# Weighing both halves of a gated chunk in one vector operation over two PSUM banks

## The chip, the cores and the metric

The kernel runs on one core of one Trainium2 chip. The metric is the device time of one launch in microseconds (us), and the time given for the kernel is the median of its runs. Beside them stands one profiled execution, from which all the rows below come.

## The reference

A stack of four layers works on `x` of 8 sequences x 128 tokens x 128 features. Each layer adds an attention (or recurrent) part and a feed-forward part, both behind a layer norm and scaled by `tanh` of a gain. The feed-forward part of the third layer is a mixture of 64 experts with 96 hidden features each, of which each token takes 8. It is the one that matters here; the kernel calls it the second mixture (m = 1; the first mixture, m = 0, is layer one's, and the third, m = 2, is layer four's).

```python
def _L2_ffn_ref(hidden_states, gate_w, w_gate, w_up, w_down):
    logits = x @ gate_w.T
    scores = softmax(logits)
    topk_w, topk_ids = top_k(scores, 8)
    topk_w = topk_w / (topk_w.sum(axis=-1, keepdims=True) + 1e-20)
    ...
    g = ragged_dot(sorted_tokens, swapaxes(w_gate, 1, 2), group_sizes)
    u = ragged_dot(sorted_tokens, swapaxes(w_up, 1, 2), group_sizes)
    h = silu(g) * u
    out = ragged_dot(h, swapaxes(w_down, 1, 2), group_sizes)
    ...
    y = (unsorted.reshape(B * S, 8, D) * topk_w[..., None]).sum(axis=1)
```

## The kernel before, in words

**Layout.** All 1024 tokens lie along the free dimension, cut into two halves of 512 columns (`HALF`), since a matmul fills one PSUM bank of 512 fp32 values per partition. The mixture is computed densely: every expert for every token, with a weight of zero where a token doesn't take the expert. The 64 x 96 = 6144 hidden features are cut into 48 chunks of 128 features (`CH2`), so that a chunk touches two experts. Products are made in fp16 with split operands: a value is a high fp16 part plus a low fp16 part, and a product is three matmuls (high x high, high x low, low x high; `three`, `products`, whose matmuls all stand at L200).

**One chunk c of the second mixture.** Banks 0 and 1 hold the gate product of the two halves, banks 2 and 3 the up product, banks 4 and 5 the hidden values, banks 6 and 7 the sum of the down products.
- SP (`moe1_sp`): loads the weights of the tokens for the chunk's rows, 2 or 3 DMAs into the buffer `WB` of 128 x 1024 (L1073), the up weights of chunk c + 2 (L1058) and the down weights of chunk c (L1064). Before the load into `WB` it waits until chunk c - 2 has been weighed (L1069, L1070).
- POOL (`moe1_pool`): splits the up weights (L906, L908) and the down weights (L918, L920) into high and low parts.
- TensorE (`moe1_pe`), in this order: the up product of chunk c (6 matmuls, behind the gate of chunk c - 1, which frees banks 2 and 3), the gate product of chunk c + 1 (6), the down product of chunk c - 1 (6, behind its low parts).
- ACT (`moe1_act`), in this order: two silus of chunk c + 1 into SBUF (L985), then for each half of chunk c the high fp16 part of the weighed values, from PSUM into SBUF (`moe_act_high`, L1016).
- DVE (`moe_dve`, m = 1): `moe1_dve_gate` multiplies silu and up product of both halves in one operation of 128 x 1024, from SBUF and banks 2 and 3 into banks 4 and 5 (L1036); `moe1_dve_weigh` multiplies banks 4 and 5 in place by `WB`, one operation of 128 x 512 for each half (L1049); `moe_dve_low` subtracts the high part from each half and writes the low part (L1186).

**What sets the order.** Each engine runs its own list in order, and semaphore counts tie the lists together. Around the change these are `w1_gated` (a chunk is gated), `w1_first` and `w1_second` (first and second half of a chunk are weighed), `e_high` and `e_low` (high and low part of a half are written; two each per chunk). The gate of chunk c waits for both low parts of chunk c - 1 (L1034), as it overwrites the banks that these read. ACT's copy of the first half waits for `w1_first`, that of the second half for `w1_second` (L1009).

**The first two chunks** are another case in the code: their gated values go to SBUF (`HF`), and the weights of the tokens come from a matmul into banks 4 and 5 (`moe1_pe_select`), so they are weighed half by half at L1044. The other 46 chunks take the branch of L1047 to L1050. All but the first two and the last two chunks run in a hardware loop of two chunks per turn.

Of the kernel before, what the change touches and what calls it, by code (L numbers as in the profile page):

```python
# [10 lines left out]
HALF = TOK // 2  # L11
# [27 lines left out]
def gated_mix_program(nc, t, out):  # L39
    fp32, fp16, bf16 = mybir.dt.float32, mybir.dt.float16, mybir.dt.bfloat16  # L40
    i32, u32 = mybir.dt.int32, mybir.dt.uint32
    ALU, ACT, AX = mybir.AluOpType, mybir.ActivationFunctionType, mybir.AxisListType.X

    ctx = ExitStack()
    with ctx:
# [5 lines left out]
        def sem(name):  # L51
            if name not in sems:
                sems[name] = ctx.enter_context(nc.semaphore(name))
            return sems[name]
# [73 lines left out]
        def bank(i, n=1):  # L128
            return PS[:, 512 * i:512 * (i + n)]
# [4 lines left out]
        def piece(at, n, dt=fp32, parts=128):  # L134

            view = SHARED[0:parts, at:at + (n if dt in (fp32, i32) else n // 2)]
            return view if dt == fp32 else view.bitcast(dt)
# [45 lines left out]
        WB = [piece(at, 1024) for at in (8192, 9216)]  # L183
# [19 lines left out]
        def settled(eng, name):  # L203

            eng.sem_inc(sem("settled_" + name), 1)
# [781 lines left out]
        def moe1_act(act):  # L987

            def step(c, u):
                if not (isinstance(c, int) and c == CH2 - 1):  # L990
                    moe1_act_silu(act, c + 1, 1 - u)
                if isinstance(c, int) and c == 0:
                    moe1_rows_act(act)
                for hf in range(2):
                    moe_act_high(act, 1, c, u, hf)
            moe1_act_silu(act, 0, 0)
            step(0, 0)
            step(1, 1)
            with act.Fori(1, CH2 // 2 - 1) as i:
                step(2 * i, 0)  # L1000
                step(2 * i + 1, 1)
            step(CH2 - 2, 0)
            step(CH2 - 1, 1)

        def moe_act_high(act, m, c, u, hf, early=False):
            M = MOE[m]
            a = M["at"] + c
            if m == 1:
                act.wait_ge(sem("w1_second" if hf else "w1_first"), c + 1)  # L1009
            elif m == 2:  # L1010
                act.wait_ge(sem("e_hidden"), 2 * c + hf + 1)
            else:
                act.wait_ge(sem("e_act"), 2 * a + hf + 1)
            if not early:
                act.wait_ge(sem("e_down"), 2 * a - 4 + hf + 1)
            act.activation(HHI[:, u, hf, :], (bank(4 + hf), HF[:, hf, :])[m // 2] if m else RH[u][:, hf, :], ACT.Copy).then_inc(sem("e_high"), 1)  # L1016
# [21 lines left out]
        def moe1_dve_weigh(dve, c, u, h):  # L1038

            dve.wait_ge(sem("w1_gated"), c + 1)  # L1040
            if isinstance(c, int) and c < 2:
                for hf in range(2):
                    dve.wait_ge(sem("w1_spread"), 2 * c + hf + 1)
                    dve.tensor_tensor(bank(4 + hf), HF[:, hf, :], bank(4 + hf), ALU.mult)\  # L1044
                        .then_inc(sem("w1_second" if hf else "w1_first"), 1)
                return
            dve.wait_ge(sem(f"w1_in{u}"), 32 * h)  # L1047
            for hf in range(2):
                dve.tensor_tensor(bank(4 + hf), bank(4 + hf), WB[u][:, HALF * hf:HALF * hf + HALF], ALU.mult)\  # L1049
                    .then_inc(sem("w1_second" if hf else "w1_first"), 1)  # L1050

        SPANS = (((0, 96, 0), (96, 128, 1)), ((0, 64, 1), (64, 128, 2)), ((0, 32, 2), (32, 128, 3)))

# [12 lines left out]
        def moe1_sp_weights(sp, c, ex, k):  # L1066

            if not (isinstance(c, int) and c < 4):
                sp.wait_ge(sem("w1_first"), c - 1)  # L1069
                sp.wait_ge(sem("w1_second"), c - 1)  # L1070
            for lo, hi, j in SPANS[k % 3]:
                settled(sp, "sp")
                sp.dma_start(WB[k % 2][lo:hi, :], t["w1"][bass.ds(ex + j, 1), :].to_broadcast([hi - lo, TOK]))                    .then_inc(sem(f"w1_in{k % 2}"), 16)  # L1073

        def moe1_sp(sp):
            moe1_sp_up(sp, 0, 0)
            moe1_sp_up(sp, 1, 1)
            moe1_sp_down(sp, 0, 0)
            moe1_sp_up(sp, 2, 0)
            moe1_sp_down(sp, 1, 1)  # L1080
            sp.wait_ge(sem("w1_rows"), 2)
            sp.dma_start(t["w1"], WROWS).then_inc(sem("w1_out"), 16)
            moe1_sp_up(sp, 3, 1)
            sp.wait_ge(sem("w1_out"), 16)

            def step(c, ex, k, up=True, down=True):
                moe1_sp_weights(sp, c, ex, k)
                if up:
                    moe1_sp_up(sp, c + 2, k % 2)
                if down:  # L1090
                    moe1_sp_down(sp, c, k % 2)
            for k in range(2, 6):
                step(k, 4 * (k // 3), k)
            with sp.Fori(1, CH2 // 6 - 1) as i:
                for k in range(6):
                    step(6 * i + k, 8 * i + 4 * (k // 3), k)
            for k in range(6):
                c = CH2 - 6 + k
                step(c, 4 * (c // 3), k, up=k < 4)
# [148 lines left out]
        def moe0_act(act):  # L1248
            act.wait_ge(sem("ld_late"), 16 * len(LATE))

            def step(c, u, h, ex, k):
                static = isinstance(c, int)
                if static and k == 2:
                    route_act(act, 0)
                for hf in range(2):
                    moe_act_silu(act, 0, c, u, hf, first=static and c < 2)
                    moe_act_high(act, 0, c, u, hf, early=static and c < 2)
            experts(act, step)
# [77 lines left out]
        def moe_act(act, m):  # L1336
            n = MOE[m]["n"]
            if m == 0:
                moe0_act(act)
                return  # L1340

            def step(c, u, h):
                for hf in range(2):
                    moe_act_silu(act, m, c, u, hf)
                for hf in range(2):
                    moe_act_high(act, m, c, u, hf)
            if m == 1:
                moe1_act(act)
            else:
                chunks(act, m, step)  # L1350
            for i in range(2):
                act.wait_ge(sem("e_down"), 2 * (MOE[m]["at"] + n) - 1 + i)
                act.activation(YS[:, HALF * i:HALF * i + HALF], bank(6 + i), ACT.Copy).then_inc(sem("y_out"), 1)

        def moe_dve(dve, m):
            n = MOE[m]["n"]

            def step(c, u, h):
                if m == 1:
                    moe1_dve_gate(dve, c, u)  # L1360
                    moe1_dve_weigh(dve, c, u, h)
                else:
                    for hf in range(2):
                        moe_dve_hidden(dve, m, c, u, hf)
                for hf in range(2):
                    moe_dve_low(dve, m, c, u, hf)
            if m == 0:
                moe0_dve(dve)
            else:
                chunks(dve, m, step)  # L1370
# [867 lines left out]
```

## Time and profile before

| | us |
|---|---|
| median of 3 runs | 690.68 |
| lowest, highest | 690.38, 695.28 |
| profiled execution, its own time | 693.94 |
| its span in the trace | 692.2 |
| granted TensorE clock, mean over the span | 0.946 |

The span is the time from the first to the last instruction in the trace; 1.74 us of the profiled execution lie around it. The profiled execution is one of its own, 3.3 us above the median of the runs. In the rows PE is TensorE's matmuls, PEld its weight loads, DVE the vector engine, ACT the scalar engine, POOL GpSimd, SP the engine that only issues DMAs here; "busy" is time with an instruction running, L1049 is line 1049 of the kernel. A granted clock of 1.00 is 2.4 GHz, 0.50 is 1.2 GHz.

### The profile page before, as it was taken

The page shows a single profiled execution, that of the slowest core. Times are in us where ns is not written, and L with a number is a line of the kernel's source. Part 1 is how long each engine was busy: PE and PEld are TensorE (multiplying, and loading weights), DVE is VectorE, ACT ScalarE, POOL GpSimd, SP SyncE. Part 2 cuts the span into 40 slices and gives each one's busy share as a digit, 9 for nine tenths or more (in the row PEclk, how much of TensorE's full clock was granted, in tenths as well). Part 3 has the DMA queues.
Part 4 walks back from the last instruction along what each step waited for, and adds up shares of the span by engine and source line. Part 5 has one row for each costly group of instructions (what it writes and reads, how often), then busy time and mean ns, then how long its engine had stood idle before and what let it go on. Part 6 is the DMA issues. An engine that isn't in the chain of part 4 may idle for free.

```text
span 692.2 us, 16594 instructions
## 1 busy us (share of the span) xinstructions
PE 601.3 (87%) x5065; PEld 284.3 (41%) x5065; DVE 551.4 (80%) x1139; ACT 370.5 (54%) x677; POOL 307.3 (44%) x592
## 2 busy tenths in 40 slices
PE   3877899999688788998699999999999789993996
PEld 2432334444256433554244444443444335551442
DVE  6684887778778895886689999999999796764797
ACT  4663788985544452334355555555555554342453
POOL 2387577772026613787425444444444100325341
PEclk9998999999889997999799999999999999996899
DMA  8000111112300000000066666656666200000110
GB/s 297 11 1 17 34 43 51 45 44 44 97 2 3 2 0 2 2 3 1 14 170 176 167 176 167 174 172 179 179 170 160 61 1 2 2 3 12 41 53 32
DMA packets 43099, 48.66 MB, mean 70 GB/s; under 512 B 7916, under 2 KB 35896, under 8 KB 42920
## 3 DMA queue, kind: packets, MB, share of 16 engines
q1 hardware_dynamic: 42616, 47.26, 24.7%
q8 instruction: 32, 0.52, 0.3%
q10 hardware_dynamic: 432, 0.73, 0.3%
q14 instruction: 19, 0.16, 0.1%
HBM read 47.14 MB, written 0.82 MB: 69 GB/s over the span
## 4 chain that ended last, share of the span: by engine, by line
DVE 41%; PE 38%; ACT 8%; POOL 6%; issue 5%; DMA 1%; DVEq 0%; ACTq 0%; POOLq 0%
PE PS L200 25%; DVE SHARED L1186 10%; DVE PS L1036 8%; DVE PS L1049 5%; ACT SHARED L1016 4%; DVE SHARED L1468 3%; PE PS L1685 2%; PE PS L1691 2%; DVE MB L1594 2%; PE PS L1572 2%; DVE REC L1699 1%; PE PS L1648 1%; DVE PS L1594 1%; POOL SHARED L1670 1%; POOL RSTD L355 1%
## 5 line engine op out<-in xcount | busy, mean ns | idle before, releaser
L200 PE MATMUL PS<-XH,UH 128*128 128x512 f16 x296 | 114.2, 386 | 7.3 <-DVE PS L1036 2.9
L200 PE MATMUL PS<-SHARED,DNH 128*128 128x512 f16 x360 | 107.5, 380 | 8.7 <-DVE SHARED L1186 8.6
L200 PE MATMUL PS<-XL,UH 128*128 128x512 f16 x296 | 113.6, 384 | 0.0
L200 PE MATMUL PS<-XH,UL 128*128 128x512 f16 x296 | 113.5, 383 | 0.0
L1016 ACT ACTIVATE SHARED<-PS 128x512 f16<-128x512 f32 x96 | 57.1, 597 | 70.7 <-DVE PS L1049 67.1
L918 POOL CAST DNH<-DF 128x128 f16<-128x128 f32 x90 | 31.8, 354 | 142.0 <-DMA DF<-in_down 97.4
L1666 ACT ACTIVATE SHARED<-PS 128x512 f32<-128x512 f32 x96 | 52.3, 595 | 71.6 <-PE PS L200 50.1
L1186 DVE TENSOR_TENSOR SHARED<-SHARED 128x512 f16<-128x512 f32 x84 | 62.6, 752 | 20.3 <-ACT SHARED L1016 19.6
L200 PE MATMUL PS<-SHARED,DNL 128*128 128x512 f16 x180 | 68.5, 380 | 0.0
L1186 DVE TENSOR_TENSOR SHARED<-PS,SHARED 128x512 f16<-128x512 f32 x96 | 62.0, 686 | 6.8 <-ACT SHARED L1016 3.4
L985 ACT ACTIVATE SHARED<-PS 128x512 f32<-128x512 f32 x96 | 57.2, 597 | 17.5 <-PE PS L200 14.8
L1016 ACT ACTIVATE SHARED<-SHARED 128x512 f16<-128x512 f32 x84 | 52.9, 630 | 22.1 <-DVE SHARED L1028 17.2
L1049 DVE TENSOR_TENSOR PS<-PS,SHARED 128x512 f32<-128x512 f32 x92 | 59.7, 694 | 4.0
L1036 DVE TENSOR_TENSOR PS<-SHARED,PS 128x1024 f32<-128x1024 f32 x46 | 56.5, 1229 | 5.3 <-PE PS L200 0.6
L908 POOL TENSOR_TENSOR UL<-UF,UH 128x256 f16<-128x256 f32 (+1 forms) x90 | 57.0, 634 | 7.2
L200 PEld LDWEIGHTS PS<-SHARED,DNH 128*128 128x128 f16 x360 | 33.0, 97 | 56.7 <-issue 21.1
L200 PEld LDWEIGHTS PS<-XH,UH 128*128 128x128 f16 x296 | 29.1, 98 | 63.6 <-DVE PS L1036 23.8
L1594 DVE TENSOR_REDUCE MB<-PS 128x4 f16<-128x512 f32 x64 | 41.1, 687 | 15.3 <-PE PS L200 11.0
L906 POOL CAST UH<-UF 128x256 f16<-128x256 f32 (+1 forms) x90 | 40.8, 454 | 27.4 <-PE PS L200 24.2
L1670 POOL TENSOR_TENSOR SHARED<-SHARED,GPT 128x512 f32<-128x512 f32 x32 | 40.0, 1273 | 26.9 <-ACT SHARED L1666 26.9
L1461 ACT ACTIVATE SHARED<-PS,LOB,LOM 128x512 f16<-128x512 f32 x48 | 35.4, 776 | 29.1 <-PE PS L200 28.9
L976 ACT ACTIVATE SHARED<-PS,B 128x512 f32<-128x512 f32 x64 | 43.4, 678 | 12.0 <-PE PS L200 9.3
(283 smaller groups left out, 1172.5 us busy)
## 6 DMA issues: line engine op xcount, KB each, us to landing
SHARED<-w_rows_dram SPq DMA_DIRECT2D x31, 384.0 KB, 3.7
SHARED<-w_rows_dram SPq DMA_DIRECT2D x30, 256.0 KB, 3.9
UF<-in_up SPq DMA_DIRECT2D x58, 128.0 KB, 3.4
DF<-in_down SPq DMA_DIRECT2D x90, 64.0 KB, 2.7
SHARED<-w_rows_dram SPq DMA_DIRECT2D x31, 128.0 KB, 2.7
UF<-in_up SPq DMA_DIRECT2D x32, 64.0 KB, 1.8
SHARED<-t_values_dram SPq DMA_DIRECT2D x2, 1024.0 KB, 10.6
SHARED<-in_masks SPq DMA_DIRECT2D x1, 1024.0 KB
```

What stands on the lines that cost most here:

```text
L200: last = pe.matmul(dst, l, r, start=start and i == 0, stop=stop and i == len(pairs) - 1)
L906: pool.tensor_copy(UH[:, u, 0:n], UF[:, u, 0:n]).then_inc(sem("e_up_ready"), 1)
L908: pool.tensor_tensor(UL[:, u, 0:n], UF[:, u, 0:n], UH[:, u, 0:n], ALU.subtract)\
L976: act.activation(RH[u][:, hf, :], bank(hf), ACT.Relu, bias=B1[:, bass.ds(c, 1)]).then_inc(sem("e_act"), 1)
L985: act.activation(SG1[u][:, hf, :], bank(hf), ACT.Silu).then_inc(sem("e_act"), 1)
L1016: act.activation(HHI[:, u, hf, :], (bank(4 + hf), HF[:, hf, :])[m // 2] if m else RH[u][:, hf, :], ACT.Copy).then_inc(sem("e_high"), 1)
L1036: dve.tensor_tensor(dst, SG1[u].rearrange("p i n -> p (i n)"), bank(2, 2), ALU.mult).then_inc(sem("w1_gated"), 1)
L1049: dve.tensor_tensor(bank(4 + hf), bank(4 + hf), WB[u][:, HALF * hf:HALF * hf + HALF], ALU.mult)\
L1186: dve.tensor_tensor(HLO[:, u, hf, :], src, HHI[:, u, hf, :], ALU.subtract).then_inc(sem("e_low"), 1)
L1594: dve.tensor_reduce(dst, src, AX, ALU.max, negate=True).then_inc(sem("a_max"), 1)
L1666: act.activation(PF[:, j, :], bank(2 + j % 2), ACT.Exp).then_inc(sem("a_exp"), 1)
L1670: pool.tensor_tensor(PG[:, j, :].rearrange("p (g s) -> p g s", g=4), PF[:, j, :].rearrange("p (g s) -> p g s", g=4), over(GPT[:, b, :], 4) ...
```

## The change

In chunks 2 to 47 DVE weighs banks 4 and 5 in one operation of 128 x 1024 in place of two of 128 x 512. It has one increment, on `w1_second`. ACT's copies of both halves wait for `w1_second` there; in chunks 0 and 1 the first half's copy still waits for `w1_first`. SP's wait for `w1_first` ahead of the load into `WB` goes, and the wait for `w1_second` stays.

```diff
@@ -1006,7 +1006,7 @@
             M = MOE[m]
             a = M["at"] + c
             if m == 1:
-                act.wait_ge(sem("w1_second" if hf else "w1_first"), c + 1)
+                act.wait_ge(sem("w1_first" if hf == 0 and isinstance(c, int) and c < 2 else "w1_second"), c + 1)
             elif m == 2:
                 act.wait_ge(sem("e_hidden"), 2 * c + hf + 1)
             else:
@@ -1045,9 +1045,7 @@
                         .then_inc(sem("w1_second" if hf else "w1_first"), 1)
                 return
             dve.wait_ge(sem(f"w1_in{u}"), 32 * h)
-            for hf in range(2):
-                dve.tensor_tensor(bank(4 + hf), bank(4 + hf), WB[u][:, HALF * hf:HALF * hf + HALF], ALU.mult)\
-                    .then_inc(sem("w1_second" if hf else "w1_first"), 1)
+            dve.tensor_tensor(bank(4, 2), bank(4, 2), WB[u], ALU.mult).then_inc(sem("w1_second"), 1)
 
         SPANS = (((0, 96, 0), (96, 128, 1)), ((0, 64, 1), (64, 128, 2)), ((0, 32, 2), (32, 128, 3)))
 
@@ -1066,7 +1064,6 @@
         def moe1_sp_weights(sp, c, ex, k):
 
             if not (isinstance(c, int) and c < 4):
-                sp.wait_ge(sem("w1_first"), c - 1)
                 sp.wait_ge(sem("w1_second"), c - 1)
             for lo, hi, j in SPANS[k % 3]:
                 settled(sp, "sp")
```

## Rows read from the trace of the kernel before

**Rows 1.** The page, part 1: busy us of each engine, share, instructions.

```profile
PE 601.3 (87%) x5065; PEld 284.3 (41%) x5065; DVE 551.4 (80%) x1139; ACT 370.5 (54%) x677; POOL 307.3 (44%) x592
```

**Rows 2.** One window: length, busy PE, PEld, DVE, ACT, POOL; clock, DMA share, GB/s.

```profile
354.00:546.00 192.00, 184.79 (x823) 76.88 (x822) 175.48 (x230) 108.97 (x183) 77.96 (x178) 1.00 0.62 167
```

**Rows 3.** Groups by line, 354 to 546: count | busy us, mean ns | idle before, releaser.

```profile
L1049 DVE TENSOR_TENSOR PS<-PS,SHARED 128x512 f32<-128x512 f32 x92 | 59.7, 694 | 4.0
L1186 DVE TENSOR_TENSOR SHARED<-PS,SHARED 128x512 f16<-128x512 f32 x92 | 59.3, 686 | 6.7 <-ACT SHARED L1016 3.4
L1036 DVE TENSOR_TENSOR PS<-SHARED,PS 128x1024 f32<-128x1024 f32 x46 | 56.5, 1229 | 5.3 <-PE PS L200 0.6
...
L1016 ACT ACTIVATE SHARED<-PS 128x512 f16<-128x512 f32 x92 | 54.7, 597 | 67.1 <-DVE PS L1049 67.1
```

**Rows 4.** Lines 1036 and 1044 alone: ns min/median/max, first and last start us.

```profile
L1036 DVE TENSOR_TENSOR PS<-SHARED,PS x46: 1228/1229/1230, 354.2 to 541.1; 128x1024 f32<-128x1024 f32 x46
...
L1044 DVE TENSOR_TENSOR PS<-SHARED,PS x4: 695/695/696, 346.1 to 351.5; 128x512 f32<-128x512 f32 x4
```

**Rows 5.** The chain that ended last, from 416: start us, length us, piece.

```profile
416.57 1.24 DVE PS L1036
...
417.84 0.71 DVE PS L1049
...
418.65 0.60 ACT SHARED L1016
...
419.28 1.30 DVE SHARED L1186 x2
...
420.67 1.24 DVE PS L1036
...
421.94 0.05 DVEq L1047
...
422.04 0.71 DVE PS L1049
...
422.86 0.60 ACT SHARED L1016
...
423.49 1.30 DVE SHARED L1186 x2
...
424.88 1.24 DVE PS L1036
```

**Rows 6.** Waits from 354 to 546: who for whom, us, times, longest.

```profile
ACT SHARED L1016 <- DVE PS L1049: 67.1, 46, 2.8
PEld PS L200 <- DVE PS L1036: 23.8, 41, 0.6
```

**Rows 7.** Timeline from 420 to 426: start us, length us, instruction, idle before.

```profile
420.53 0.43 POOL L920 TENSOR_TENSOR DNL<-DF,DNH 128x128 f16<-128x128 f32 x1
...
421.95 0.10 PEld L200 LDWEIGHTS PS<-XH,UH 128*128 128x128 f16 x1 [0.53 <-DVE PS L1036]
...
422.04 1.30 DVE L1049 TENSOR_TENSOR PS<-PS,SHARED 128x512 f32<-128x512 f32 x2
...
424.56 0.59 PE L200 MATMUL PS<-SHARED,DNH 128*128 128x512 f16 x2
...
425.63 0.38 PE L200 MATMUL PS<-SHARED,DNL 128*128 128x512 f16 x1
```

**Rows 8.** The page, part 6: DMA issues, KB each, us to landing.

```profile
SHARED<-w_rows_dram SPq DMA_DIRECT2D x30, 256.0 KB, 3.9
```

**Rows 9.** A window with the columns of rows 2; then timeline of PE.

```profile
80.00:100.00 20.00, 18.10 (x80) 7.05 (x79) 18.59 (x36) 15.43 (x25) 14.18 (x27) 1.00 0.14 41
...
83.37 0.59 PE L200 MATMUL PS<-SHARED,DNH 128*128 128x512 f16 x2 [0.85 <-DVE SHARED L1186]
...
641.06 0.63 PE L200 MATMUL PS<-XL,UH 128*128 128x512 f16 x1
641.49 0.63 PE L200 MATMUL PS<-XH,UL 128*128 128x512 f16 x1
```

## The prediction, made before the change was run

> **What bounds the kernel now.** I started with the totals [rows 1]: TensorE is busy for 87% of the span and DVE for 80%. That would make DVE's work look half covered, so the next view is the second mixture's own stretch [rows 2], which holds all 46 chunks that the change touches. There both are busy almost throughout (184.79 and 175.48 of 192 us, TensorE's clock granted in full), and the totals cannot say which one sets the pace.
>
> The chain of waits can [rows 5]. It never passes through TensorE in this stage. It goes round one ring, once per chunk: DVE gates both halves (L1036), DVE weighs the first half (L1049), ACT copies that half to fp16 (L1016), DVE takes the two low parts (L1186), and then the gate of the next chunk. The steps of two chunks, start to start:
> - gate to weighing: 1.27 (417.84 - 416.57) in one chunk, 1.37 (422.04 - 420.67) in the next, where a piece of DVE's own sequencer at L1047 stands in between (421.94);
> - weighing to ACT's copy: 0.81 and 0.82;
> - ACT's copy to the low parts: 0.63 and 0.63;
> - low parts to the next gate: 1.39 and 1.39.
> Together 4.10 and 4.21, mean 4.155 us. The first and last of the 46 gates start at 354.2 and 541.1 [rows 4]: 186.9 / 45 = 4.15, so the ring describes the whole stage.
>
> Two things must be seen in this ring. The gate of the next chunk can't run ahead, because it writes the two banks that the low parts still read. And ACT's copy starts behind the first half alone: the second half runs from about 422.66 to 423.34 (the pair takes 1.30 from 422.04 [rows 7]), while ACT works from 422.86. The second half's weighing is almost wholly beside ACT's first copy.
>
> TensorE waits for this ring: its first weight load of a chunk had stood idle 0.53 us until the gate's end [rows 7], and such waits add up to 23.8 us [rows 6]. Its 18 matmuls follow each other at (425.63 - 421.95) / 17 = 0.216 us [rows 7], so they need 3.9 of the 4.155.
>
> **The change, part by part.**
>
> *DVE's work.* 46 times (chunks 2 to 47) two weighings of 512 columns, 694 ns each [rows 3], become one over 1024. The trace has no weighing over two banks in place. It has the gate, over two banks from SBUF and PSUM into PSUM, fp32, at 1229 ns with a spread of 2 ns [rows 4]. Working in place costs nothing that rows show: the weighing of 512 in place takes 694 with PSUM as its first operand and 695 with PSUM as its second [rows 3, 4]. I take 1.23 us. The bounds: no longer than two single operations end to end, 2 x 0.694 = 1.39, if a second bank started afresh; no shorter than one single operation, 0.69, if it ran at twice the gate's rate, for which no row speaks. Busy time thus falls from 59.7 to 46 x 1.229 = 56.5 us. From first start to last end it falls from 1.30 to 1.23.
>
> *ACT's wait.* In the loop both halves' copies now wait for the one increment at the operation's end. What ended 0.694 after the start now ends 1.229 after it. The term is 1.229 - 0.694 = 0.535 us per chunk; with the bounds of the operation it lies between 0 and 0.69. The handing over to ACT (0.81 - 0.69 = 0.12) stays. Queued behind ACT's waiting instruction are the second copy and the two silus of two chunks ahead, which the gate needs a whole turn later; ACT waited 67.1 us for the weighing already, 46 times [rows 6], and its four operations take 4 x 0.597 = 2.4 us [rows 3] of a chunk, so nothing there becomes late.
>
> *Is anything of it covered?* DVE has nothing to do in the added wait: behind the weighing in its queue stand the low parts, which need ACT's copy, then the gate, which needs the banks. The second copy finishes 0.597 behind the first and the second low part starts about 0.6 behind the first, now as before; so the second half gives nothing back. The whole 0.535 is on the ring.
>
> *DVE's waits and increments.* One increment fewer per chunk. The load's wait (L1047) and the 0.10 us more that every second chunk shows before its weighing stay, as I see no reason for them to go; if they went, it would be 23 x 0.10 = 2.3 us less.
>
> *SP.* One wait on a count falls away; the other one, for the weighing of two chunks before, remains and now comes at about the same place behind the weighing's start (1.23 instead of 1.30). SP's three kinds of DMA per chunk then go out as before. A load of the weights lands 3.9 us after issue [rows 8], and there are 2 x 4.155 - 1.30 = 7.0 us from that point to the weighing that uses it, which become 2 x 4.69 - 1.23 = 8.2. I cost it at nothing.
>
> *POOL and TensorE.* POOL's split of the down weights ended at 420.53 + 0.43 = 420.96, and the matmuls that use it began at 424.56 [rows 7]: 3.6 us of room. TensorE's down products of a chunk need the low parts, which end later against TensorE's own start: the gate's end plus 0.04 to 0.14, 1.23, 0.12, 0.63 and 0.69 give the first half ready about 2.8 us after it, when the 12 matmuls ahead (12 x 0.216 = 2.6) are done. So TensorE may idle 0.2 there and the rest at the gate, about 0.8 of the new 4.69 us in all. It isn't late.
>
> *First two chunks.* Chunks 0 and 1 keep their code and counts: nothing.
>
> *Sum.* 46 x 0.535 = 24.6 us; the ring goes from 4.155 to 4.69. Against the profiled execution: span 692.2 + 24.6 = 716.8, and with the 1.74 us around the span (693.94 - 692.2) 718.5. That execution lay 3.3 us above the runs' median of 690.68; I take the term over to the median: 715.3 us, 3.6% slower. A measurement of this kernel can tell about 1%.
>
> **A rule against a row.** Rows first: two single operations are busy 1.388 us, one double 1.229 [rows 3, 4], so 0.16 us of work per chunk goes. The Trainium skill (VectorE: DVE Perf Modes, section on the TRN2 errata) says that vector operations pay a fixed cost per instruction, so that one large tile pays it once and many small ones each time. The trace agrees on the durations; by this rule alone the merged form should win, and the sum would be that of rival A in place of the forecast.
>
> **The rivals.**
>
> *A, DVE's own work is the bound (not slower).* If the low parts started because the second weighing had ended, and not because ACT's copy had, the ring would lose 1.30 - 1.23 = 0.07 per chunk: 46 x 0.07 = 3.2 us, 687.5 us, within 1%. It decides where ACT's copy ends before the last weighing does. For it: DVE is busy 91% of the stretch [rows 2]. Against it: the copy ends at 422.86 + 0.60 = 423.46, behind the weighing's end at 423.34, and the low part starts 0.03 after the copy [rows 5, 7]; after the change the copy can't even start before 1.23 + 0.12.
>
> *B, the second bank costs afresh.* With 1.39 for the operation the term is 0.694: 46 x 0.694 = 31.9 us, 722.6. Against it stands the gate's 1229 ns, in 46 of 46.
>
> *C, TensorE's clock falls.* Its free time per chunk grows from 4.155 - 3.9 = 0.27 to 4.69 - 3.9 = 0.8, from 94% of the time in matmuls to 83%, in a stage that had the clock in full [rows 2]. At the lower level (1.2 GHz) matmuls follow each other at 641.49 - 641.06 = 0.43 us [rows 9], so 18 take 7.7 us and TensorE becomes the bound: 7.7 - 4.69 = 3.0 us more for each chunk at that level; a tenth of the 46 gives 14 us, 729, all of them 853. Against it: the first mixture has 80 matmuls in 20 us, 80 x 0.216 = 17.3 us or 86%, with a wait of 0.85 among them, and its granted clock is 1.00, the level of 2.4 GHz [rows 9]; and TensorE would be wholly busy as soon as the clock fell. The Trainium skill (TensorE: Matmul & The Clock Gate, section on psum-queue depth-cycling) warns that frequent short idles between groups of matmuls can make the clock go up and down; by it the time would be C's. The first mixture's rows show no such thing.
>
> **How the numbers follow.** The forecast holds with 0.84 (its own range 711 to 719: 46 times a term between 0.45 and 0.6 with the execution's scatter), A 0.03, B 0.08, C 0.05. The range from 710 to 722 takes in the smaller gap of L1047 below and most of B above. Slower by over 1%: forecast, B and C, and what A doesn't take, 0.96; within 1%: 0.03, case A; faster by over 1%: 0.01, for which no case stands beyond an unlikely faster operation in A.
>
> **What would show it.** Right: one weighing of 128x1024 at 1.23 us, 46 times; ACT's copy about 1.35 after its start; DVE idle some 0.7 us before the low part, released by ACT, 46 times, so about 30 us in place of the 3.4 of before [rows 3]; a ring of 4.6 to 4.75 us; the clock at 1.00 in the stage; everything outside it unchanged. Wrong: a ring still near 4.1 (A), an operation near 1.39 (B), matmuls 0.43 apart in the stage (C), or a low part that starts in front of its copy.

## The result, and the profile after

The changed kernel takes 716.36 us (median of 4 runs, 714.61 to 719.81) against 692.93 for the kernel before beside it: ratio 1.0345, 95% interval 1.0281 to 1.0409. It is slower, by 23.4 us at these medians; 715.3 and a term of 24.6 us had been forecast. The profiled execution took 714.61 us with a span of 712.8. In the changed kernel the weighing stands at L1048 and the low parts at L1183.

The stage first, as a window with the columns of [rows 2]. It is 19 us longer than the window of before, and it leaves out 1.8 us at the front, as the first gate now stands at 352.2; from the first to the last of the 46 gates the stage takes 210.9 us in place of 186.9:

```profile
354.00:565.00 211.00, 188.87 (x808) 68.80 (x805) 168.93 (x181) 94.56 (x179) 76.91 (x176) 1.00 0.57 151
```

TensorE's clock is still granted in full over the whole of it. Now the groups by line from 354 to 567, as in [rows 3]:

```profile
L1183 DVE TENSOR_TENSOR SHARED<-PS,SHARED 128x512 f16<-128x512 f32 x92 | 59.3, 686 | 34.2 <-ACT SHARED L1016 34.2
L1048 DVE TENSOR_TENSOR PS<-PS,SHARED 128x1024 f32<-128x1024 f32 x46 | 56.7, 1232 | 4.0
...
L1016 ACT ACTIVATE SHARED<-PS 128x512 f16<-128x512 f32 x92 | 49.9, 594 | 116.1 <-DVE PS L1048 116.1
```

The weighing has become what it was to become: 46 operations of 1232 ns, 56.7 us in place of 59.7. DVE does 3 us less work, and yet it now waits 34.2 us for ACT before the low parts, where it waited 3.4. The single line of the gate gives the length of the ring (ns min/median/max, first and last start), to be held against [rows 4]:

```profile
L1036 DVE TENSOR_TENSOR PS<-SHARED,PS x46: 1229/1229/1230, 352.2 to 563.1; 128x1024 f32<-128x1024 f32 x46
```

(563.1 - 352.2) / 45 = 4.69 us, where it was 4.15. The chain of waits shows which steps grew; its rows answer to [rows 5]:

```profile
413.16 1.24 DVE PS L1036
...
414.42 1.24 DVE PS L1048
...
415.76 0.60 ACT SHARED L1016
...
416.39 0.54 DVE SHARED L1183
...
417.79 1.24 DVE PS L1036
...
419.05 0.05 DVEq L1047
...
419.15 1.24 DVE PS L1048
...
420.51 0.60 ACT SHARED L1016
```

Gate to weighing 1.26 and 1.36, as before. Weighing to ACT's copy 1.34 and 1.36, where it was 0.81 and 0.82. Copy to low part 0.63, low parts to gate 1.40: as before. One step of four has changed, and by the 0.54 us by which an operation of 1024 columns ends later than one of 512 (1.232 - 0.694). TensorE's side, from the timeline (start, length, instruction, idle before):

```profile
421.46 0.38 PE L200 MATMUL PS<-XH,UL 128*128 128x512 f16 x1
...
421.89 0.60 PE L200 MATMUL PS<-SHARED,DNH 128*128 128x512 f16 x2
...
423.00 0.38 PE L200 MATMUL PS<-SHARED,DNL 128*128 128x512 f16 x1
...
423.82 0.39 PE L200 MATMUL PS<-XH,UH 128*128 128x512 f16 x1 [0.43 <-DVE PS L1036]
```

Beyond the 0.216 from one matmul to the next it loses 421.89 - 421.46 - 0.22 = 0.21 us ahead of the down products and 423.82 - 423.00 - 0.22 = 0.60 at the gate. In the chunk before this one, where nothing stands at L1047, the two are 0.09 and 0.59.

### The profile page after: what moved, and what is told of

Its sections match the earlier page's. It is cut to its first block, busy times and chain, and to the rows that moved or that the text cites. A ratio compares the mean times of both kernels' runs of the same rounds, so it can differ in the third digit from the quotient of the medians.

```text
span 712.8 us, 16548 instructions
## 1 busy us (share of the span) xinstructions
PE 604.3 (85%) x5065; PEld 276.4 (39%) x5065; DVE 548.6 (77%) x1093; ACT 358.9 (50%) x677; POOL 306.8 (43%) x592
## 4 chain that ended last, share of the span: by engine, by line
DVE 44%; PE 36%; ACT 8%; POOL 6%; issue 5%; DVEq 1%; DMA 1%; ACTq 0%; POOLq 0%
PE PS L200 23%; DVE SHARED L1183 9%; DVE PS L1048 8%; DVE PS L1036 8%; ACT SHARED L1016 4%; DVE SHARED L1465 3%; PE PS L1682 2%; PE PS L1688 2%; PE PS L1569 2%; DVE MB L1591 2%; DVE PS L1591 1%; DVE REC L1696 1%; PE PS L1645 1%; DVE STAT L343 1%; POOL SHARED L1667 1%
## 5 line engine op out<-in xcount | busy, mean ns | idle before, releaser
L1016 ACT ACTIVATE SHARED<-PS 128x512 f16<-128x512 f32 x96 | 52.3, 595 | 119.6 <-DVE PS L1048 116.1
L1183 DVE TENSOR_TENSOR SHARED<-PS,SHARED 128x512 f16<-128x512 f32 x96 | 62.0, 686 | 34.3 <-ACT SHARED L1016 34.2
L1663 ACT ACTIVATE SHARED<-PS 128x512 f32<-128x512 f32 x96 | 52.1, 595 | 69.4 <-PE PS L200 48.9
L1183 DVE TENSOR_TENSOR SHARED<-SHARED 128x512 f16<-128x512 f32 x84 | 62.8, 753 | 21.3 <-ACT SHARED L1016 20.7
L1036 DVE TENSOR_TENSOR PS<-SHARED,PS 128x1024 f32<-128x1024 f32 x46 | 56.5, 1229 | 5.3 <-PE PS L200 0.6
L908 POOL TENSOR_TENSOR UL<-UF,UH 128x256 f16<-128x256 f32 (+1 forms) x90 | 56.7, 630 | 7.2
L1048 DVE TENSOR_TENSOR PS<-PS,SHARED 128x1024 f32<-128x1024 f32 x46 | 56.7, 1232 | 4.0
L985 ACT ACTIVATE SHARED<-PS 128x512 f32<-128x512 f32 x96 | 55.1, 605 | 4.6 <-PE PS L200 4.3
L200 PEld LDWEIGHTS PS<-SHARED,DNH 128*128 128x128 f16 x360 | 27.0, 97 | 72.2 <-issue 32.9
```

Of the source, the lines that this page charges most:

```text
L200: last = pe.matmul(dst, l, r, start=start and i == 0, stop=stop and i == len(pairs) - 1)
L908: pool.tensor_tensor(UL[:, u, 0:n], UF[:, u, 0:n], UH[:, u, 0:n], ALU.subtract)\
L985: act.activation(SG1[u][:, hf, :], bank(hf), ACT.Silu).then_inc(sem("e_act"), 1)
L1036: dve.tensor_tensor(dst, SG1[u].rearrange("p i n -> p (i n)"), bank(2, 2), ALU.mult).then_inc(sem("w1_gated"), 1)
L1048: dve.tensor_tensor(bank(4, 2), bank(4, 2), WB[u], ALU.mult).then_inc(sem("w1_second"), 1)
L1183: dve.tensor_tensor(HLO[:, u, hf, :], src, HHI[:, u, hf, :], ALU.subtract).then_inc(sem("e_low"), 1)
```

## The experiments

Each ratio is to the kernel before on the same chip, with its 95% interval; the rings are worked out from the first and last start of the gates, as above.

**1. The wait alone** (`wait_only`). The two weighings stay; ACT's first copy waits for the second of them.

```diff
-                act.wait_ge(sem("w1_second" if hf else "w1_first"), c + 1)
+                act.wait_ge(sem("w1_first" if hf == 0 and isinstance(c, int) and c < 2 else "w1_second"), c + 1)
```

> Two weighings of 512 columns as in the kernel before; only ACT's copy of the first half waits for the second weighing. Theory (the ring passes through ACT's copy, and what counts is when that copy is released): the release moves from 0.694 to 1.30 us after the weighing's start, so the ring goes from 4.155 to 4.76 us and the kernel becomes 46 x 0.606 = 28 us slower, more than by the changed kernel. Rival (the operation over two banks, or DVE's busy time, is what costs): DVE's work is untouched, so no more than 2 us either way.

Measured: 721.4 us, ratio 1.0435 (1.0382 to 1.0488), 0.0435 x 693 = 30 us slower. The gate's line:

```profile
L1036 DVE TENSOR_TENSOR PS<-SHARED,PS x46: 1228/1230/1230, 353.2 to 567.2; 128x1024 f32<-128x1024 f32 x46
```

The ring is (567.2 - 353.2) / 45 = 4.76, as expected. DVE's operations are those of the kernel before, and the kernel is slower than the changed one, in which the pair's end comes 0.07 us sooner. Both kernels wait for the second half and only the changed one has the wide operation: the wait is the cause.

**2. A wait half as long** (`cut768`).

```diff
-            for hf in range(2):
-                dve.tensor_tensor(bank(4 + hf), bank(4 + hf), WB[u][:, HALF * hf:HALF * hf + HALF], ALU.mult)\
-                    .then_inc(sem("w1_second" if hf else "w1_first"), 1)
+            for k, (lo, hi) in enumerate(((0, 768), (768, 2 * HALF))):
+                dve.tensor_tensor(bank(4, 2)[:, lo:hi], bank(4, 2)[:, lo:hi], WB[u][:, lo:hi], ALU.mult)\
+                    .then_inc(sem("w1_second" if k else "w1_first"), 1)
```

> Two weighings, cut at column 768 in place of 512: the first covers bank 4 and half of bank 5. The waits are those of the kernel before. Theory: the first operation takes 0.694 + 256 columns at (1.229 - 0.694) / 512 us each = 0.96 us, so ACT's copy is released 0.267 us later; the ring goes to 4.42 and the kernel becomes 46 x 0.267 = 12.3 us slower, half of what the changed kernel costs. Rival (two banks in one operation cost by themselves): the whole 24 us already, as the first operation spans two banks. Rival (DVE's busy time alone): no change.

Measured: 704.2 us, ratio 1.0186 (1.0142 to 1.0229), 0.0186 x 693 = 13 us slower. The groups by line, and the gate's line:

```profile
L1186 DVE TENSOR_TENSOR SHARED<-PS,SHARED 128x512 f16<-128x512 f32 x92 | 59.3, 687 | 19.0 <-ACT SHARED L1016 19.0
...
L1049 DVE TENSOR_TENSOR PS<-PS,SHARED 128x768 f32<-128x768 f32 x45 | 43.5, 967 | 3.8
L1049 DVE TENSOR_TENSOR PS<-PS,SHARED 128x256 f32<-128x256 f32 x45 | 19.0, 423 | 0.0
```

```profile
L1036 DVE TENSOR_TENSOR PS<-SHARED,PS x46: 1230/1230/1230, 351.3 to 550.4; 128x1024 f32<-128x1024 f32 x46
```

The ring is (550.4 - 351.3) / 45 = 4.42, as expected. Releases at 0.694, 0.967, 1.232 and 1.30 us after the weighing's start give rings of 4.15, 4.42, 4.69 and 4.76: each 0.1 us of later release is 0.1 us of ring. An operation that reaches into a second bank costs nothing besides its columns: 256 more take 0.273 us across the border of the banks (694 to 967 ns) and 0.265 behind it (967 to 1232).

**3. SP's wait alone** (`sp_only`): the line `sp.wait_ge(sem("w1_first"), c - 1)` goes, nothing else.

> The kernel before with SP's wait for the first weighing taken away and nothing else. Theory: no change, within 1 us or what the runs scatter; the ring stays at 4.155. Rival (SP's sequencer or the time at which the loads go out matters): the ring moves by 0.05 us or more.

Measured: 690.91 us, ratio 0.9981 (0.9960 to 1.0001), not to be told from no change; the gates start from 353.1 to 540.2, a ring of 4.16.

**4. The wait covered** (`ahead_fused`). The wide weighing stays, but, against the changed kernel, the gate of the next chunk goes to SBUF (`HF`) and stands between the weighing and the low parts. Only the weighing now waits for the low parts of the chunk before. TensorE's down products come one chunk later, and POOL's down split with them.

```diff
-            dst = HF.rearrange("p i n -> p (i n)") if isinstance(c, int) and c < 2 else bank(4, 2)
-            dve.tensor_tensor(dst, SG1[u].rearrange("p i n -> p (i n)"), bank(2, 2), ALU.mult).then_inc(sem("w1_gated"), 1)
+            dve.tensor_tensor(HF.rearrange("p i n -> p (i n)"), SG1[u].rearrange("p i n -> p (i n)"), bank(2, 2), ALU.mult).then_inc(sem("w1_gated"), 1)
...
+            dve.wait_ge(sem("e_low"), 2 * (CH0 + c))
+            dve.tensor_tensor(bank(4, 2), HF.rearrange("p i n -> p (i n)"), WB[u], ALU.mult).then_inc(sem("w1_second"), 1)
...
-                        moe_pe_down(pe, 1, c - 1, 1 - u, hf, start=static and c == 1)
+                        moe_pe_down(pe, 1, c - 2, u, hf, start=static and c == 2)
...
                     moe1_dve_weigh(dve, c, u, h)
+                    if not (isinstance(c, int) and c == CH2 - 1):
+                        moe1_dve_gate(dve, c + 1, 1 - u)
```

> The changed kernel's single weighing of 1024 columns, but the gate of the next chunk now goes to SBUF and stands on DVE between the weighing and the low parts, so that DVE works while ACT copies; down products run one chunk later on TensorE, and POOL's down split moves with them. Theory: with cover for the wait the single operation costs nothing: DVE's chunk is 1.27 + 1.15 + 1.29 + 0.10 to 0.2 = 3.8 to 3.9 us, TensorE's 18 x 0.216 = 3.9 us, so a ring of 3.9 to 4.1 us and a kernel 3 to 12 us faster than before, DVE no longer idle before the low parts. Rival (the single operation or its two banks cost by themselves, or TensorE's order becomes late): a ring of 4.4 us or more, slower than before.

Measured: 681.08 us, ratio 0.9849 (0.9800 to 0.9898), 10 us faster than before. The groups by line:

```profile
L1188 DVE TENSOR_TENSOR SHARED<-PS,SHARED 128x512 f16<-128x512 f32 x94 | 60.3, 683 | 0.7 <-ACT SHARED L1016 0.7
L1051 DVE TENSOR_TENSOR PS<-SHARED 128x1024 f32<-128x1024 f32 x46 | 57.9, 1258 | 4.0
```

DVE waits 0.7 us for ACT in the whole stage, and the ring is 3.89 us (gates of chunks 2 and 47 at 353.80 and 528.62). The wide weighing no longer holds the ring up once there is work behind it that needs no copy.

**5. The same order on DVE alone** (`ahead_nolag`): as 4, but TensorE's down products and POOL's down split keep their old places.

> As ahead_fused in DVE's order, but TensorE's down products and POOL's down split stay where they are in the kernel before. Theory: TensorE becomes late. Its down products of chunk c wait for low parts that now stand behind the gate of chunk c + 1, and the up product of chunk c + 2, which that gate's successor needs, stands behind them: ring about gate 1.2 + low part 0.7 + down 1.3 + up 1.3 and some 0.2 of handing over = 4.6 to 4.7 us, so some 20 to 25 us slower than before, about as slow as the changed kernel. Rival (only DVE's order matters): about as fast as ahead_fused.

Measured: 719.39 us, ratio 1.0383 (1.0342 to 1.0425), 27 us slower. DVE's timeline:

```profile
423.13 1.22 DVE L1038 TENSOR_TENSOR SHARED<-SHARED,PS 128x1024 f32<-128x1024 f32 x1 [1.02 <-PE PS L200]
424.27 1.28 DVE L1186 TENSOR_TENSOR SHARED<-PS,SHARED 128x512 f16<-128x512 f32 x2
425.69 1.23 DVE L1051 TENSOR_TENSOR PS<-SHARED 128x1024 f32<-128x1024 f32 x1
427.84 1.22 DVE L1038 TENSOR_TENSOR SHARED<-SHARED,PS 128x1024 f32<-128x1024 f32 x1 [0.92 <-PE PS L200]
```

No wait for ACT, but 0.9 to 1.0 us at each gate for the up product, which stands behind the down product on TensorE; ring 4.71. Cover on one engine has to be followed through the others.

**6. Two weighings in the covered order** (`ahead_split`), beside the fused kernel once more (`ahead_fused_b`), and both with less work for TensorE (`light_fused`, `light_split`). `ahead_split` weighs each half from `HF` in an operation of its own, and ACT's first copy waits for the first of them. The light kernels leave out the product of the down weights' low part with the values' high part: 16 matmuls per chunk, as in this line.

```diff
             products(pe, bank(at + hf), three(DNH[:, u, :], DNL[:, u, :], HHI[:, u, hf, :], HLO[:, u, hf, :])[:2 if m == 1 else 3],
```

> The same kernel as ahead_fused, beside ahead_split on one chip. Both theories: a ratio of about 0.985 again, ring 3.88 us, set by TensorE.

> As ahead_fused, but with the weighing as two operations of 512 columns (last end 0.07 us later) and ACT's first copy released by the first of them. Theory (with the gate between, the copy is covered either way, and TensorE's 3.9 us set the pace): within 1 us of ahead_fused. Rival (a single weighing costs wherever it stands): ahead_split 5 us or more faster. Rival (DVE still sets the pace): ahead_split 46 x 0.07 = 3 us slower.

> As ahead_fused, but the second mixture's down product leaves out the matmul of the down weights' low part with the high part of the values: 16 matmuls per chunk, 3.45 us, so that TensorE no longer sets the pace. Theory: DVE's own work does, ring 3.75 to 3.85 us, 1 to 6 us faster than ahead_fused.

> As ahead_split, with the same part of the down product left out as in light_fused. Here DVE's work is the bound and ACT's copy is covered, the condition of the prediction's rival A. Theory: the ring is 0.05 to 0.1 us longer than light_fused's, so light_split is 2 to 5 us slower than light_fused: in this place one operation in place of two pays. Rival (one operation is worse in any place): light_split faster.

| kernel | us | ratio | interval | ring, us |
|---|---|---|---|---|
| ahead_fused_b | 681.5 | 0.9848 | 0.9817 to 0.9880 | 3.93 |
| ahead_split | 688.19 | 0.9933 | 0.9907 to 0.9959 | 4.06 |
| light_fused | 682.58 | 0.9864 | 0.9832 to 0.9895 | 3.90 |
| light_split | 690.4 | 0.9963 | 0.9946 to 0.9981 | 4.04 |

Three expectations missed. The split form is not within 1 us of the fused one but 6.7 us slower. `light_split` is 7.8 us slower than `light_fused` and its ring 0.14 longer, where 2 to 5 us and at most 0.1 had been expected. And the kernels with 16 matmuls are no faster than those with 18, where 1 to 6 us had been expected: TensorE was no tighter a bound than DVE. (The weighing of `light_fused` took 1.29 us in the mean against 1.26 in `ahead_fused`; how much that hides of what the shorter list of matmuls gives is not shown.) The two weighings were longer than in the kernel before. The groups by line of `light_split`:

```profile
L1052 DVE TENSOR_TENSOR PS<-SHARED 128x512 f32<-128x512 f32 x92 | 65.7, 758 | 4.0
```

758 ns where it was 694. In this order the weighing reads both its operands from SBUF. The timeline of `ahead_split` has a pair that takes 1.57 us in place of 1.30, begun in the same moment as a split of POOL's:

```profile
425.86 0.43 POOL L920 TENSOR_TENSOR DNL<-DF,DNH 128x128 f16<-128x128 f32 x1
425.87 1.57 DVE L1052 TENSOR_TENSOR PS<-SHARED 128x512 f32<-128x512 f32 x2
```

and that of `ahead_fused` has a cast of POOL's, begun inside a wide weighing, that takes 1.28 us in place of 0.29 and ends 0.15 us behind the weighing:

```profile
426.39 1.23 DVE L1051 TENSOR_TENSOR PS<-SHARED 128x1024 f32<-128x1024 f32 x1
...
426.49 1.28 POOL L918 CAST DNH<-DF 128x128 f16<-128x128 f32 x1 [0.76 <-PE PS L200]
```

**7. POOL's work taken away** (`thin_fused`, `thin_split`). Both build on the light kernels. Inside the hardware loop POOL splits only 8 columns of the up and down weights, and TensorE multiplies older values for the rest.

```diff
             a, n = M["at"] + c, 256 if M["gated"] else 128
+            if m == 1 and not isinstance(c, int):
+                n = 8
...
+            n = 8 if m == 1 and not isinstance(c, int) else 128
+            pool.tensor_copy(DNH[:, u, 0:n], DF[:, u, 0:n]).then_inc(sem("e_down_ready"), 1)
```

> As light_fused, and in the hardware loop of the second mixture POOL splits only 8 columns of the up and down weights (TensorE reads older values for the rest), so that POOL hardly works beside DVE. Theory (DVE's weighing from two SBUF operands and POOL's splits hold each other up): every weighing of 1024 columns takes 1.23 us, where light_fused has a mean of 1.29; ring 3.84 us against 3.90. Rival (the weighing's varying length has another cause, such as DMA): mean stays at 1.29.

> As light_split, with POOL's splits cut down in the same way. Theory: the two weighings of 512 columns go back to about 0.695 us each (0.758 in light_split), pair 1.30, ring 3.91 us against light_split's 4.04, 0.07 us above thin_fused: that 46 x 0.07 = 3 us is what one operation saves by itself where ACT's copy is covered, and the rest of the 6 to 8 us between the split and fused kernels was POOL. Rival (POOL is not the cause): mean stays near 0.76, ring near 4.04.

Measured: 681.01 us, ratio 0.9829 (0.9792 to 0.9865), and 682.7 us, ratio 0.9855 (0.9815 to 0.9894). The weighings by line, fused and then split:

```profile
L1054 DVE TENSOR_TENSOR PS<-SHARED 128x1024 f32<-128x1024 f32 x46 | 56.8, 1234 | 4.0
```

```profile
L1055 DVE TENSOR_TENSOR PS<-SHARED 128x512 f32<-128x512 f32 x90 | 58.6, 696 | 3.8
```

Both are back at their plain lengths. The rings are 3.84 (gates of chunks 2 and 47 at 354.15 and 527.1) and 3.91 (353.42 and 529.4), 0.07 apart. That is also the difference of the operations themselves, as the pair of `thin_split` takes 1.30 us from first start to last end. This is what one operation in place of two is worth by itself when DVE is the bound, 46 x 0.07 = 3 us; the rings of the light pair are 0.14 apart, and without POOL's work half of that is gone. The medians differ by 1.7 us and the two ratios' intervals overlap, so this rests on the rings and the lengths. Each ring is that of one execution: those of `ahead_fused` and `ahead_fused_b`, the same kernel, are 0.04 apart.

## Why the prediction was right

**The bound.** The ring of four steps was read rightly: it gave 4.155 us before, and experiments 1 and 2 moved only the release of ACT's copy and found the ring where the sum put it, to 0.01 us. The totals would have misled: DVE does less work in the changed kernel and the kernel is slower.

**The operation's length.** 1.23 us taken from the gate, 1.232 measured. The trace of before had no such operation, but one alike in banks, columns and type was the row to go by. Working in place and a second bank cost nothing that shows (1232 ns against the gate's 1229), so rival B falls.

**The term.** 0.535 us per chunk were forecast; the profiled rings differ by 4.69 - 4.15 = 0.53, and 45 turns of that are 24.0 us. The spans differ by 712.8 - 692.2 = 20.6 only: the changed kernel's stage began 2.0 us earlier (first gate at 352.2 against 354.2), and what follows the last gate is 149.7 us against 151.1. The latter is mostly one wait, DVE's for TensorE at the stage's end, 2.78 us against 4.46; the granted clock there was 1.00 in the one execution (566 to 573) and 0.66 in the other (546 to 550). The same wait was 4.5 in `sp_only`, 5.72 in `wait_only` and 2.77 in `ahead_fused`, so it doesn't go with the length of the ring. Both parts are taken as scatter between executions; as each kernel has one trace, or two, that is argued and not shown. The ratio's interval stands for 19 to 28 us, so it is in part luck that the medians differ by 23.4, so near the sum's 24.6; the finer test of the forecast is the ring, 0.53 us for 0.535.

**What did not cover it.** SP's dropped wait changed nothing (experiment 3). TensorE idled 0.21 us ahead of the down products and 0.60 at the gate (0.09 and 0.59 in the other chunk of a turn of the loop), where 0.2 and the rest of about 0.8 had been forecast. The 0.10 us at L1047 in every second chunk stayed. DVE's wait was 34.2 us for the "about 30" forecast: 46 x 0.74.

**Rival A** needs ACT's copy off the ring. It wasn't there, and in experiment 7, where it is, the price that the prediction gave it holds: 0.07 us per chunk. Of the 0.16 us of busy time that the merged form saves (2 x 0.694 - 1.232), 0.09 had been overlap of the two operations already, as the pair took 1.30 and not 1.39. So the Trainium skill's rule that a large tile pays the fixed cost once (VectorE: DVE Perf Modes, section on the TRN2 errata) is right about the operation, and the place in the ring decides the time.

**Rival C.** The clock did not fall: TensorE's share of time in matmuls went from 94% to 83% and the stage stayed at 1.00. In `ahead_nolag` it was 18 x 0.216 / 4.71 = 83% too, and also 1.00.

**The chances.** The forecast, B and C are all slower by over 1% and add up to 0.97, where the prediction wrote 0.96; nothing hangs on it.

## What to carry to other kernels

A merged operation releases whoever waited for its first half only when all of it is done: before merging two operations look up who waits for the first of them, and whether the producing engine has other work until that waiter is done. If the waiter is on the ring, the merge costs in each turn what the second half adds to the operation, here 0.54 us, though it saves busy time. Where it is wanted all the same, put independent work behind the merged operation first, and follow the new order through every engine; here that gave the fastest of the kernels that leave nothing out, 1.5% below the kernel before.

## What was not expected

A vector operation with two SBUF operands and POOL's casts and subtractions hold each other up: DVE's 512 columns went from 0.696 us (`thin_split`, POOL's splits cut to 8 columns) to 0.758 in the mean and 0.975 at the longest (`light_split`), and POOL's cast of 128 x 128 from 0.289 us to a mean of 1.08 in `ahead_fused`. With one operand in PSUM, as in this stage of the kernels before and after, the lengths of DVE's weighings and low parts spread by 16 ns at most. The Trainium skill (SBUF — State Buffer, section on who interferes with whom) states that a vector instruction with two SBUF inputs contends with GpSimd instructions that read SBUF; experiment 7 agrees. So does `ahead_nolag`, where POOL does its full work but its splits fall beside DVE's idle time, gate and low parts: there the weighing from two SBUF operands took 1.232 to 1.235 us in all 46 chunks and the cast 0.29 in the mean. The kernel before shows the like in its first mixture, whose low parts read two SBUF operands: they took 0.736 us in the mean where this stage's take 0.686, and the cast of 128 x 128 took 0.470. Two short operations suffered more than one long one: in a pair the second operation can find POOL in its way again, which is argued from the timelines and was not tried by itself. A version that keeps the gate ahead and one operand in PSUM was not tried either.
